# A four-stage attention kernel: masks of the third stage written by TensorE instead of VectorE and GpSimd, and one spacing for the filling work

## What is computed

```
x = x + attn_masked(norm(x));  x = x + ffn0(norm(x))   # stage MASKED: softmax over keys >= query
x = x + attn_rbf(norm(x));     x = x + ffn0(norm(x))   # stage RBF: exp(-r * |q - k|^2), no softmax
x = x + attn_rel(norm(x));     x = x + ffn1(norm(x))   # stage REL: relative positions, softmax
x = x + attn_rope(norm(x));    x = x + ffn1(norm(x))   # stage ROPE: rotated q and k, softmax
```

```
term1 = q . k ; term2 = q . r ; term3 = u . k ; term4 = v . r
scores = (term1 + term3 + rel_shift(term2 + term4)) / sqrt(8)

def rel_shift(x):                      # x: B, H, S, L
    x = pad(x, one column on the left)
    return x.reshape(B, H, L + 1, S)[:, :, 1:S + 1, :]
```

## Time and profile before

| | us |
|---|---|
| median of 3 runs | 2883.49 |
| lowest, highest | 2878.53, 2889.88 |
| profiled execution: its own time | 2889.88 |
| profiled execution: its span | 2888.2 |

### The profile page before, as it was taken

The page is one execution under the profiler, slowest core; times in us unless marked ns, Lnnn a source line. Parts: engine busy times, 40 slices in busy tenths (PEclk is TensorE's granted clock), DMA queues, the critical chain, the costliest instruction groups (busy, mean ns, idle before and its releaser), DMA issues.

```text
span 2888.2 us, 107431 instructions
## 1 busy us (share of the span) xinstructions
PE 2666.9 (92%) x43168; PEld 1575.8 (55%) x43168; DVE 2080.3 (72%) x5639; ACT 2106.0 (73%) x3765; POOL 982.7 (34%) x2453
## 2 busy tenths in 40 slices
PE   4999999999999999999999999889999999999995
PEld 2666665655556545566666566556544444444443
DVE  3888888722212228888788878878889989999993
ACT  1777776799999976666666666556677878878774
POOL 3212223322303424834753573463314132140111
PEclk9999999999999989999999999999999999999997
DMA  6324242343323432411321231222123223232221
GB/s 172 97 84 118 84 115 77 113 123 111 118 86 119 128 110 65 123 49 56 97 86 49 80 111 53 76 70 73 45 62 100 63 68 90 68 105 65 65 66 32
DMA packets 197639, 250.60 MB, mean 87 GB/s; under 512 B 48196, under 2 KB 113604, under 8 KB 197144
## 3 DMA queue, kind: packets, MB, share of 16 engines
q1 hardware_dynamic: 197144, 243.73, 28.7%
HBM read 133.25 MB, written 100.14 MB: 81 GB/s over the span
## 4 chain that ended last, share of the span: by engine, by line
PE 64%; DVE 18%; issue 8%; POOL 4%; ACT 3%; SPq 2%; DMA 1%; DVEq 0%; ACTq 0%; POOLq 0%
PE ppv L960 28%; DVE mx L1217 11%; PE ring L830 5%; PE ring L808 5%; PE ring L822 5%; PE ring L867 4%; PE ring L900 3%; PE pm L991 2%; ACT probs L1095 2%; DVE seen L1201 2%; DVE seen L1212 2%; PE ring L916 1%; PE pm L1044 1%; PE pm L976 1%; PE pm L1035 1%
## 5 line engine op out<-in xcount | busy, mean ns | idle before, releaser
L1095 ACT ACTIVATE probs<-ring 128x512 f32<-128x512 f32 (+1 forms) x3280 | 1971.8, 685 | 709.1 <-PE ring L822 355.8
L1217 DVE TENSOR_REDUCE mx<-ring 128x1 f32<-128x512 f32 (+2 forms) x2112 | 1288.6, 650 | 260.6 <-PE ring L867 107.3
L960 PE MATMUL ppv<-probs,values 128*32 128x128 f32 x30208 | 1160.7, 279 | 25.8 <-POOL probs L1479 18.2
L960 PEld LDWEIGHTS ppv<-probs,values 128*32 128x32 f32 x30208 | 798.6, 110 | 347.2 <-issue 192.5
L1212 DVE CUSTOM_DVE_ANT_0 seen<-ring,low_seen 128x512 f32<-128x512 f32 x576 | 392.8, 682 | 78.0 <-PE ring L867 77.5
L874 PE MATMUL ring<-kst,qst 48*128 48x512 bf16 (+1 forms) x1060 | 365.3, 391 | 43.3 <-DVE mx L1217 21.4
L830 PE MATMUL ring<-qst,kst 51*128 51x512 bf16 (+2 forms) x1092 | 353.1, 389 | 3.2 <-ACT probs L1095 1.7
L1441 POOL CAST mparts<-mall 128x8 bf16<-128x8 f32 x192 | 36.5, 190 | 874.9 <-DVE mall L1235 740.9
L867 PE MATMUL ring<-kst,qst 112*128 112x512 bf16 (+3 forms) x768 | 254.1, 331 | 19.3 <-DVE mx L1201 18.0
L1477 POOL TENSOR_SCALAR_AFFINE_SELECT probs<-probs 128x128 f32<-128x128 f32 x512 | 149.2, 292 | 334.2 <-ACT probs L1095 332.9
L822 PE MATMUL ring<-qst,kst 115*128 115x512 bf16 (+3 forms) x768 | 251.8, 328 | 0.0
(11 more groups left out here) (140 smaller groups left out, 2950.1 us busy)
## 6 DMA issues: line engine op xcount, KB each, us to landing
qst<-records_q SPq DMA_DIRECT2D x448, 96.0 KB
heads_out<-osb SPq DMA_DIRECT2D x256, 128.0 KB, 2.0
kst<-records_k SPq DMA_DIRECT2D x320, 96.0 KB
records_k<-parts SPq DMA_DIRECT2D x96, 256.0 KB, 3.3
records_q<-parts SPq DMA_DIRECT2D x96, 256.0 KB, 3.2
kst<-records_k SPq DMA_DIRECT2D x128, 102.0 KB
oT<-heads_out SPq DMA_DIRECT2D x64, 128.0 KB, 2.8
den<-inverses SPq DMA_DIRECT2D x48, 128.0 KB, 2.6
```

The lines of the kernel that those rows point to most:

```text
L960: mm = pe.matmul(ppv[32 * g:32 * g + 32, c:c + P], values[:, (n // H) % 2, v:v + 32], src[:, at * P:(at + 1) * P], start=u == 0 and qt < 4 ...
L1095: nc.scalar.activation(probs_of(rd.n, u), src, ACT.Exp, scale=1.0 if rd.s == RBF else SCALE).then_inc(s_exp, 1)
L1217: ins = dve.tensor_reduce(mx[:, slot, to:to + 1], bank[:, at * P:(at + nt) * P], AX.X, ALU.max)
```

## The change

Five edits.

1. **REL, exponentials.** `hide` and its semaphore are gone. TensorE adds the mask into the bank before ScalarE reads it: one more matmul per masked unit, with the identity as weights and a table of 0 and -1e30 as the moving operand. An upper unit gets one of 512 columns (`up_kq`). A unit with a diagonal tile gets one of 128 or 129 columns (`low_kq`); one unit (key tile 4, first half) gets one of a single column. Nine of these stand in a head.
2. **REL, row maxima.** An upper unit gets a mask matmul of 512 columns (`up_qk`), and VectorE reduces the bank with one plain `tensor_reduce` of 512 columns into four maxima, in place of four masked reductions. The sixteen other units keep L1212.
3. **REL, groups of value products** become `{6: 5 units, 10: 4, 14: 4, 19: 5}`, where they were `{6: 5, 10: 3, 14: 5, 20: 5}`; ScalarE's eviction stands at slot 2 instead of 3.
4. **The plan** puts fillings 3 slots apart and normalised tiles 1 slot apart in all stages. This moves work in intervals 4 to 6 (RBF) and 12 to 15 (ROPE).
5. Two more constant tables are loaded at the start.

```diff
@@ lag @@
     if rd.s == REL:
-        return {6: [0, 1, 2, 3, 4], 10: [5, 6, 7], 14: [8, 9, 10, 11, 12], 20: [13, 14, 15, 16, 17]}
+        return {6: [0, 1, 2, 3, 4], 10: [5, 6, 7, 8], 14: [9, 10, 11, 12], 19: [13, 14, 15, 16, 17]}
@@ Plan @@
-APART = {MASKED: 3, RBF: 6, REL: 3, ROPE: 9}
-TILES_APART = {MASKED: 1, RBF: 1, REL: 1, ROPE: 2}
...
-        self.free = tick + self.apart
+        self.free = tick + 3
...
-            self.at["xn" + w, j, i, t] = tick + t * self.tiles
-        return [tick + t * self.tiles + 2 for t in (3, 7)]
+            self.at["xn" + w, j, i, t] = tick + t
+        return [tick + 3 + 2, tick + 7 + 2]
@@ unit_kq, REL @@
                         for i, (kt, qt, _, at) in enumerate(unit):
-                            mm = pe.matmul(bank[:, at * P:(at + 1) * P], keys[rows, slot, kt * P:(kt + 1) * P],
-                                           qst_up[rows, slot, qt * P:(qt + 1) * P], start=i == 0, stop=i == len(unit) - 1)
+                            pe.matmul(bank[:, at * P:(at + 1) * P], keys[rows, slot, kt * P:(kt + 1) * P],
+                                      qst_up[rows, slot, qt * P:(qt + 1) * P], start=i == 0, stop=False)
+                        mm = pe.matmul(bank[:, :], identb[:, :], up_kq[:, :], start=False, stop=True)
                     else:
...
-                        cut = min(max(kt * P, lo), hi)
+                        cut, first = min(max(kt * P, lo), hi), kt * P - 1
+                        m0, m1 = max(first, lo), min((kt + 1) * P, hi)
...
+                        if m1 > m0:
+                            mm = pe.matmul(bank[:, m0 - lo:m1 - lo], identb[:, :], low_kq[:, m0 - first:m1 - first],
+                                           start=False, stop=True)
@@ unit_qk, REL, upper @@
+                        mm = pe.matmul(bank[:, :], identb[:, :], up_qk[:, :], start=False, stop=True)
@@ take_values @@
-                if rd.s == REL and hidden_in(rd.kq[u]):
-                    pe.wait_ge(s_up, (n - REL * HEADS) * HIDDEN + sum(hidden_in(v) for v in rd.kq[:u + 1]))
@@ scalar @@
-                    if u == (3 if stage(rd.n - 1) == REL else 2) and rd.n > 0 and stage(rd.n - 1) != RBF:
+                    if u == 2 and rd.n > 0 and stage(rd.n - 1) != RBF:
@@ maxima @@
-                    dve.wait_ge(s_sm, item - 2)
-                    for qt, _, _, at in unit:
-                        to = 2 * NT + qt
-                        ins = dve.tensor_tensor_reduce(seen[:, item % 3, at * P:(at + 1) * P], bank[:, at * P:(at + 1) * P], up_seen[:, :],
-                                                       1.0, 3.0 * BIG, ALU.add, ALU.max, mx[:, slot, to:to + 1])
-                    ins.then_inc(s_sm, 1)
+                    to = 2 * NT + unit[0][0]
+                    dve.tensor_reduce(mx[:, slot, to:to + 4], bank[:, :].rearrange("p (t q) -> p t q", t=4), AX.X, ALU.max)\
+                        .then_inc(s_sm, 1)
@@ gpsimd: hide and its calls are removed @@
-                    pool.affine_select(tile, tile, [[0, 4], [-1, P]], ALU.is_ge, 0.0, base=-2, channel_multiplier=1).then_inc(s_up, 1)
...
-                    pool.affine_select(own, own, [[1, P]], ALU.is_ge, 0.0, base=0, channel_multiplier=-1).then_inc(s_up, 1)
...
-                    pool.memset(tile[0:1, kt - q0 - 1, P - 1:P], 0.0).then_inc(s_up, 1)
```

More of the change, by code:

```diff
@@ L82, in upper @@
     return unit[0] in UPPER[0] + UPPER[1]
-def hidden_in(unit):
-    kt, q0, _, _ = unit[0]
-    return 1 if upper(unit) else (q0 <= kt < q0 + 4) + (q0 < kt <= q0 + 4)
-HIDDEN = sum(hidden_in(unit) for unit in KQ_UNITS[REL])
 @dataclass
@@ L257, in lay @@
         self.j, self.us, self.taken = j, US[j // B], set()
-        self.apart = 3 if j == REL * B - 1 else APART[j // B]
-        self.tiles = TILES_APART[j // B]
         base = ROUNDS[H * j].tick
@@ L323, in idle @@
         s = min(i, INTERVALS - 1) // B
-        self.free, self.apart = tick, 0
+        self.free = tick
         names = [(j, i, "ta", 0), (j, i, "ta", 1)] + [(j, i, "pr", n) for n in range(2 * PROJ[s])] + \
@@ L488, in build @@
         s_mp = sem("s_mp")
-        s_up = sem("s_up")
         s_zc = sem("s_zc")
@@ L745, in _ @@
             const1(heads_of[:, :], k["heads_of"])
-            for dst, n in ((low_seen, "low_seen"), (up_seen, "up_seen")):
+            for dst, n in ((low_seen, "low_seen"), (low_kq, "low_kq"), (up_qk, "up_qk"), (up_kq, "up_kq")):
                 const1(dst[:, :], k[n].bitcast(BF16))
@@ L822, in unit_kq @@
                                 mm = pe.matmul(bank[:, p0 - lo:p1 - lo], keys[rows, slot, kt * P:(kt + 1) * P],
-                                               qq[rows, slot, p0:p1], start=p0 == lo, stop=p1 == hi)
+                                               qq[rows, slot, p0:p1], start=p0 == lo, stop=p1 == hi and m1 <= m0)
+                        if m1 > m0:
+                            mm = pe.matmul(bank[:, m0 - lo:m1 - lo], identb[:, :], low_kq[:, m0 - first:m1 - first],
+                                           start=False, stop=True)
                 else:
@@ L858, in unit_qk @@
                         for i, (qt, kt, _, at) in enumerate(unit):
-                            mm = pe.matmul(bank[:, at * P:(at + 1) * P], qst_up[rows, slot, qt * P:(qt + 1) * P],
-                                           keys[rows, slot, kt * P:(kt + 1) * P], start=i == 0, stop=i == len(unit) - 1)
+                            pe.matmul(bank[:, at * P:(at + 1) * P], qst_up[rows, slot, qt * P:(qt + 1) * P],
+                                      keys[rows, slot, kt * P:(kt + 1) * P], start=i == 0, stop=False)
+                        mm = pe.matmul(bank[:, :], identb[:, :], up_qk[:, :], start=False, stop=True)
                     else:
@@ L1465, in next_values @@
                                    zexp[:, i % 2].unsqueeze(2).to_broadcast([P, NT, VCOLS]), ALU.mult).then_inc(s_zv, 1)
-            def hide(n, u):
-                unit, tile = ROUNDS[n].kq[u], probs_of(n, u).rearrange("p (t q) -> p t q", t=4)
-                pool.wait_ge(s_exp, ROUNDS[n].exps + u + 1)
-                if upper(unit):
-                    pool.affine_select(tile, tile, [[0, 4], [-1, P]], ALU.is_ge, 0.0, base=-2, channel_multiplier=1).then_inc(s_up, 1)
-                    return
-                (kt, q0, _, _), = unit
-                if q0 <= kt < q0 + 4:
-                    own = tile[:, kt - q0]
-                    pool.affine_select(own, own, [[1, P]], ALU.is_ge, 0.0, base=0, channel_multiplier=-1).then_inc(s_up, 1)
-                if q0 < kt <= q0 + 4:
-                    pool.memset(tile[0:1, kt - q0 - 1, P - 1:P], 0.0).then_inc(s_up, 1)
             def next_scores(n):
@@ L1620, in _ @@
                 for u in range(rd.slots):
-                    if u == 0 and rd.n > 0 and stage(rd.n - 1) == REL:
-                        hide(rd.n - 1, 17)
-                    if u > 0 and rd.n >= 0 and rd.s == REL and hidden_in(rd.kq[u - 1]):
-                        hide(rd.n, u - 1)
                     if u == 1:
@@ L1674, in shape_constants @@
     i = np.arange(P)
+    wide = np.arange(P + 1)
     band = np.arange(8 * P) - 3 * P
@@ L1687, in shape_constants @@
         "low_seen": hide((band[None, :] > i[:, None]) & ((band[None, :] < P) | (band[None, :] == P) & (i[:, None] == P - 1))),
-        "up_seen": hide(i[None, :] < i[:, None] + 2),
+        "low_kq": hide((wide[None, :] - 1 < i[:, None]) & ((wide[None, :] > 0) | (i[:, None] == 0))),
+        "up_qk": np.tile(hide(i[None, :] < i[:, None] + 2), (1, 4)),
+        "up_kq": np.tile(hide(i[:, None] < i[None, :] + 2), (1, 4)),
         "zmask": np.where((i[:, None] == P - 1) & (np.arange(NT)[None, :] == NT - 1), f(BIG), f(0)).astype(f),
```

4 lines of the change are left out of this document (3 added, 1 removed).

## The result

The changed kernel takes 2918.39 us, the median of 4 runs (2916.05 to 2922.97); the kernel before took 2885.29 us beside it (4 runs, 2878.53 to 2889.88). The ratio is 1.0118, with a 95% interval of 1.0094 to 1.0143: 33 us slower, where 63 us were forecast and 2913 to 2985 us was the range. The profiled execution took 2915.3 us, with a span of 2913.2, so between the two profiles lie only 25 us. I take the sums apart between profiles and say at the end how they stand to the medians.

A forecast was written before the change was run, and what follows sets the result against it. TensorE was taken as the fullest engine wherever the change lands. REL +42 (88 - 25.5 - 20), RBF +13 and ROPE +8 sum to +63 us: 2953 profiled, 2947 us median; own range 2928 to 2968, whole range 2913 to 2985.

The forecast's parts named there:

- Plain REL heads: REL heads without projection work: from 14.03 to 14.03 + 1.37 - 0.40 = 15.0 us.
- the turn's wait: REL, TensorE's wait ahead of the turned maxima (L930): its 12.3 us in 53 waits stay.
- The price of the masks: REL, added mask matmuls on TensorE: 1.37 us a head, 88 us over 64 heads if nothing hides it.
- the wait's relief: REL, TensorE's wait for VectorE's masked upper maxima (L1201) goes: 0.40 us off a steady head.
- I take 20 us off: REL, TensorE's 14 waits for GpSimd's hiding go: 17.5 us noted, 20 us with the matmul tails.
- the 25.5 behind the upper maxima: REL, all 52 waits for the masked maxima (L1201) go: 17.2 us noted, 25.5 us with tails.
- 8 us for the tiles: ROPE, normalised tiles every slot: about 1.0 us lost in each of eight groups, as ScalarE falls behind.
- I see nothing in the change that would alter that: Granted clock, 0.97 to 1.00 in the stages read, stays near the 2.4 GHz level; no time charged.
- Waits absorb more of the masks: Rival, 0.15: turn's wait goes, projection heads hide their masks; REL +20, RBF +8, ROPE 0: 2911 us.
- The dearer rival: Rival, 0.17: bunched fillings and masks in projection heads stall ScalarE and VectorE; REL +60, RBF +16, ROPE +20: 2979 us.
- the faster one: Rival, 0.06: the exponential-GpSimd-value-product round trip paces REL, 0.28 us saved per value group; REL -10, total 2873 us.
- The weight-load share: REL, 602 of 1003 us: by the skill's rule TensorE has room for the masks; start-to-start distances speak against it.

The follow-up runs named there:

- second executions: The kernel before and the changed kernel, unaltered, each profiled once more: 2889.5 and 2921.3 us.
- C2 alone: Kernel before plus only the wide TensorE mask of the upper row maxima and VectorE's plain reduction; GpSimd's hiding stays: 2886.07 us, ratio 1.0007.
- C alone: Kernel before plus all masks on TensorE (exponentials and maxima), with old value-product groups, eviction place and spacings: 2906.73 us, ratio 1.0063.
- C1 alone: Kernel before plus only the exponentials' masks on TensorE, GpSimd's hiding gone; maxima, groups and plan as before: 2894.18 us, ratio 1.0020.
- A alone: Kernel before with only the new plan, fillings 3 slots and normalised tiles 1 slot apart in every stage; REL untouched: 2899.22 us, ratio 1.0047.
- B alone: Kernel before with only the new value-product groups (5, 4, 4, 5 units) and eviction at slot 2; masks stay on VectorE and GpSimd: 2877.37 us, ratio 0.9977.

## Why the prediction was right, and where it was off

The sign, the range and the ruling mechanism held: TensorE is the full engine, and a mask on it is paid. The size was twice too large: 2918 us lies near the low end of the range and outside the forecast's own 2928 to 2968. Between the profiles the parts are, in us, forecast and measured: REL +42 and +25.3, RBF's intervals 4 to 6 +13 and +8.5, ROPE +8 and +4.9, interval 7 none and -11.6, all else 0 and -2. That is +63 and +25. By the medians it is 33, so the profile of before (4.6 us above its median) and of after (3.1 below) hide 8 us of the loss. The second executions of the two differ by 31.8 us, nearly as the medians do: REL +26.0, RBF's intervals 4 to 6 +11.4, ROPE +7.6, interval 7 -14.3. So most of the hidden part is RBF's and ROPE's, where the forecast was closer than the first pair says.

**Plain REL heads: right.** 15.0 forecast, 15.04 measured. The 32 heads from the eighth to the fifteenth of each interval, nearly all plain, went from 452.0 to 484.0 us, more than the whole loss of the stage. The wait behind the upper maxima went, the turn's wait stayed, no wait for GpSimd remained, and no new one for ScalarE came. The price of the masks (1.37 forecast, 1.24 measured) and the wait's relief (0.40 forecast, 1.24 - 1.01 = 0.23 measured) were both too high by about 0.15, and the two errors cancelled: that the sum fits to 0.04 us is luck.

**REL heads with projections: the step that failed.** "I take 20 us off" for GpSimd was the sum of the waits that name it, and the missing 17 us are in the heads that have them. In the first seven heads of each interval, 28 in all, the length went from 480.0 to 475.8 us, and in the last ones from 71.6 to 68.8. They lost 7 us, though the masks put 32 x 1.24 = 40 us into them. So 47 us of other time went. The forecast had taken off 20 for GpSimd and, of the 25.5 behind the upper maxima, the 12.7 that are not in the 32 plain heads: 33 in all. Six such heads of interval 9, before and after:

```profile
L1083 ACT ACTIVATE osb<-ppv x7: 380/380/380, 1367.0 to 1466.7; 128x256 f32<-128x256 f32 x7
```

```profile
L1072 ACT ACTIVATE osb<-ppv x7: 377/377/378, 1369.5 to 1469.8; 128x256 f32<-128x256 f32 x7
```

They took 99.7 and take 100.3 us, with 7.4 us of masks in them. One head shows what the noted waits leave out. It is the third of interval 11 in the kernel before:

```profile
1893.90:1919.50 25.60, 19.87 (x255) 13.38 (x255) 16.51 (x61) 10.39 (x22) 13.44 (x28) 0.87 0.23 67
...
1906.00:1912.00 6.00, 1.52 (x40) 1.07 (x40) 0.96 (x4) 0.00 (x0) 6.00 (x9) 0.78 0.02 5
1912.00:1919.50 7.50, 7.50 (x93) 4.59 (x86) 6.05 (x30) 4.01 (x8) 6.23 (x16) 0.72 0.26 69
```

While GpSimd worked off what stood in its queue, TensorE was busy for 1.5 of 6 us, VectorE and ScalarE ran dry with it, and the granted clock then sank to 0.72. The waits noted in that head for GpSimd are 5.2 us; the head takes 18.7 us after the change, 6.9 less, although 1.24 us were added, so 8.1 us went. The clock accounts for most of the difference: 6.8 us of the head ran at the 1.2 GHz level, worth up to 3.4 us. Over REL the time at that level fell from 20.5 to 10.2 us, at most 5 of the 47 us; 9 more, beyond those 5 and the forecast's 33, aren't traced. How much is GpSimd's shows between C2 alone and C alone, which differ in the exponentials' masks and the hiding. The 28 heads went from 475.5 to 473.2 us while receiving 26 us of masks, so 29 us went, where C2's trace notes 16.7 for GpSimd. This 29 holds the rest of L1201's and some of the turn's waits too, and again up to 5 us of the clock. C1 alone, where 41 us went, holds most of L1201's. So what failed, as far as is known, is that the noted waits were taken as the whole price of a late GpSimd: in the head shown the lower clock behind the stall came on top, and some 9 us over all 32 heads stay open.

**RBF: right.** Thirteen heads were to take 104 us and take 103.0, 3.6 us more than before. Three times that is 10.8. The profile of after shows 8.5, since its first head of interval 4 took 6.5 us and that of before 9.1, with 7 us at half clock; in the changed kernel's second execution it took 9.1 too, again with 7 us at half clock, and the three intervals 377.0 us, 11 more than before.

**ROPE: near in size, the reason not shown.** I charged nothing for bunched fillings and 8 us for the tiles. The five heads with the fillings went to 63.8 us, against "near 60", and the fillings that had stood among the later heads are gone from those. The stage loses 4.9 us between the first profiles and 7.6 between the second; at full clock an interval loses 2.8, so the first three 8.4. Whether that is of tiles or of fillings wasn't tried apart; A alone gives the same heads.

**Interval 7: not foreseen.** "I see nothing in the change that would alter that", on the clock, failed, and it made the loss smaller by 12 to 14 us. By which edit, or why, isn't known. Of the 38 us between the forecast's sum and the measured 25, 17 are REL's and 11.6 are here; RBF, ROPE and the rest make the other 9.

**The rivals.** "Waits absorb more of the masks" was the nearest with 2911 us: the projection heads do hide their masks, and by that half it was right; the turn's wait didn't go, by which it was wrong. The dearer rival and the faster one fell. The latter wanted over 88 us of waits to go in REL; 88 - 25 = 63 went. The weight-load share named with it (602 of 1003 us, the Trainium skill's "Trainium Kernel Development and Optimization", section "Performance Expectations") would have left room for the masks; in plain heads nine tenths of their price were paid.

## What to carry to other kernels

Where an engine that only helps (here GpSimd, with selections of 0.28 us behind projections of 2 us in one queue) is sometimes late, its noted waits need not be its whole price, for a stall can bring a lower clock behind it: look at the length of the heads in which it is late against those in which it isn't. An added matmul in a steady stretch of the fullest engine costs nearly its start-to-start distance (1.24 of 1.39 us here), and a wait ahead of a change between bf16 scores and fp32 value products is partly hidden in that change, so taking the wait away brings less than it shows. Compare a stage's granted clock between the two kernels before you give a gain to an edit: 12 us of this case's sum came that way, and a stage whose code is the same differed by 15 us between profiles.

## What the runs showed of the hardware

- The same wait of 1.3 us in a full stream was followed by 24 to 34 us at the 1.2 GHz level in six profiles and by none or 3 us in seven. What tells them apart stays open: B alone has the kernel before's instruction order up to that place, and only its groups in REL, which comes later, differ. Once there, the level stayed although TensorE was busy without a gap (18.00 of 18 us at 0.50).
- TensorE's change from a 512-column bf16 matmul to fp32 value products or a transpose took 0.31 us start to start, 0.22 between two of the first kind. A matmul of one column took 0.03, one of 128 columns 0.06.
- All 128 matmul records of one line (L801) were missing from a trace, while its weight loads were there at 97 ns each and its time could be read between its neighbours.
